# A decoder layer's expert stage: row numbers and gates on GpSimd, the gate as the scale of each dot product

## What is computed

```python
q = (x @ Wq.T).reshape(b, n, 2, HEADS, DIM_KEY).transpose(2, 0, 1, 3, 4)   # HEADS = 8
sim = jnp.einsum('pbnhd,hkpd->pbnhk', q, keys)                              # 128 keys
...                                          # best of the pairs: scores, indices (TOPK = 1)
A_in, B_in = in_a[indices], in_b[indices]
A_out, B_out = out_a[indices], out_b[indices]
gate = jax.nn.relu(scores)
hidden = x @ W_in.T
lin = jnp.einsum('bnd,bnhkd->bnhk', x, A_in) * gate
hidden = hidden + jnp.einsum('bnhk,bnhkd->bnd', lin, B_in)
hidden = jax.nn.gelu(hidden, approximate=False)
out = hidden @ W_out.T
lout = jnp.einsum('bnd,bnhkd->bnhk', hidden, A_out) * gate
out = out + jnp.einsum('bnhk,bnhkd->bnd', lout, B_out)
```

## Time and profile before

| | us |
|---|---|
| median of 3 runs | 2556.84 |
| lowest and highest | 2553.26, 2561.50 |
| span of the profiled execution | 2553.4 |
| VectorE busy in the span | 2042.5 (80%) |
| TensorE busy in the span | 2402.2 (94%) |
| GpSimd busy in the span | 1079.4 (42%) |

### The profile page before, as it was taken

One profiled execution on the slowest core, in us unless ns is written; L12 is line 12 of the kernel. 1 busy time (PEld: TensorE's weight loads), 2 busy tenths in 40 slices (PEclk: granted clock), 3 DMA queues, 4 the chain that ended last, 5 costly groups with the idle time before them and its releaser, 6 DMA issues. The chain is left out here.

```text
span 2553.4 us, 40781 instructions
## 1 busy us (share of the span) xinstructions
PE 2402.2 (94%) x12856; PEld 1333.3 (52%) x12856; DVE 2042.5 (80%) x5966; ACT 1121.9 (44%) x2612; POOL 1079.4 (42%) x1564
## 2 busy tenths in 40 slices
PE   7889999999999999999989899999999999999985
PEld 5456666656666566666555344444444444444432
DVE  1467776677767776677665699999999999999997
ACT  2257666667666666667666122222122222212221
POOL 1133333333333333334233445555555555555552
PEclk9999999999999999999999999999999999999998
DMA  3035554455545545455458789999999999999996
GB/s 112 15 108 139 163 151 141 134 148 149 155 125 144 162 143 155 114 145 172 135 148 258 272 337 390 392 382 384 382 382 383 385 389 391 383 383 382 385 371 261
DMA packets 292741, 622.47 MB, mean 244 GB/s; under 512 B 162352, under 2 KB 163376, under 8 KB 292528
## 3 DMA queue, kind: packets, MB, share of 16 engines
q0 software_dynamic: 83968, 438.34, 45.2%
q1 hardware_dynamic: 174768, 80.85, 11.9%
q10 hardware_dynamic: 33792, 100.67, 11.7%
HBM read 577.80 MB, written 142.61 MB: 282 GB/s over the span
## 5 line engine op out<-in xcount | busy, mean ns | idle before, releaser
L1544 POOL DMA_INDIRECT out_rows<-rows_out,rows_now x256 | 272.0, 1063 | 373.1 <-PE out_ps L1611 292.5
L1054 ACT ACTIVATE in_rows<-scores,nmx 128x512 f32<-128x512 f32 x512 | 373.2, 729 | 113.8 <-DVE nmx L1243 111.1
L1565 PE MATMUL l_bank<-fold,xn_tf 128*128 128x512 f32 x960 | 421.6, 592 | 0.0
L1060 ACT COPY in_rows<-t_bank 128x512 f32<-128x512 f32 x512 | 298.7, 584 | 214.7 <-PE t_bank L715 213.7
L1535 POOL DMA_INDIRECT in_rows<-rows_in,rows_now x248 | 303.2, 1223 | 128.9 <-DVE hid L1799 63.8
L622 POOL TENSOR_TENSOR added<-mask_add,band 128x136 f32<-128x136 f32 (+1 forms) x512 | 246.7, 483 | 256.4 <-DVE nmx L1243 255.0
L715 PE MATMUL t_bank<-ident,in_rows 128*128 128x128 f32 x2048 | 319.6, 281 | 10.1 <-ACT in_rows L1027 5.1
L715 PEld LDWEIGHTS t_bank<-ident,in_rows 128*128 128x128 f32 x2048 | 237.4, 143 | 171.6 <-issue 100.8
L683 PE MATMUL a_bank<-fold 128*128 128x256 f32 (+1 forms) x1024 | 303.9, 441 | 15.4 <-ACT fold L975 6.9
L1807 DVE CUSTOM_DVE_ANT_0 out_rows<-out_rows,hid 128x1024 f32<-128x1024 f32 x256 | 307.1, 1221 | 3.5 <-ACT hid L1668 3.5
L1655 ACT COPY sims<-l_bank 128x512 f32<-128x512 f32 x120 | 70.2, 585 | 537.2 <-PE l_bank L1565 516.9
(11 more groups left out here) (210 smaller groups left out, 3829.9 us busy)
## 6 DMA issues: line engine op xcount, KB each, us to landing
rows_in<-in_in_b_dram ACTq DMA_DIRECT2D x16, 2048.0 KB, 8.5
rows_out<-in_out_a_dram ACTq DMA_DIRECT2D x16, 2048.0 KB, 9.0
rows_in<-in_in_a_dram ACTq DMA_DIRECT2D x16, 1024.0 KB, 8.3
rows_out<-in_out_b_dram ACTq DMA_DIRECT2D x16, 1024.0 KB, 5.8
rel_scratch<-rel_pad SPq DMA_DIRECT2D x16, 640.0 KB, 3.2
band<-rel_scratch SPq DMA_DIRECT2D x512, 20.0 KB, 2.5
prob_scratch<-in_rows SPq DMA_DIRECT2D x512, 20.0 KB, 2.3
near<-prob_scratch SPq DMA_DIRECT2D x64, 156.1 KB, 3.1
```

The source lines that it names most:

```text
L1054: nc.scalar.activation(prob_tile(s % PSLOTS), scores[:, s % 2, :], ACT.Exp, bias=nmx[:, s:s + 1], scale=-1.0, accum_out=lsum[:, s:s + 1]). ...
L1060: nc.scalar.copy(prob_t[:, n // HPT % 2, n % HPT, :, :].rearrange("p k q -> p (k q)"), bank[:]).then_inc(t_emptied, 1)
L1544: nc.gpsimd.indirect_dma_start(out_rows[:, h, :], None, rows_out, bass.IndirectOffsetOnAxis(rows_now[:, odd, h:h + 1], 0)).then_inc(out_lo ...
L1565: ins = nc.tensor.matmul(l_bank[c % 2][:], xn_t[:, k, :], fold[:, k, c * BANK:(c + 1) * BANK], start=(k == 0), stop=(k == KD - 1))
```

## The change

Row numbers, score sums and gates are no longer made on VectorE. GpSimd makes them in a new `pick`, in six instructions on 128x8 (the multiply-and-add of the row number is now a multiply, a conversion and an addition), with waits on a counter `row_step` of its own. It stands between the input gathers of a round and its output gathers, and serves the next round. `gates` and `rows_now` now have four places, as many as the ring of tokens, and the copy of `rows` is gone.

The five multiplies by the gate are gone too. Each of the 16 products takes `gates[:, slot, h:h + 1]`, one value per partition, as its scale, where it had the constant 1.0. ScalarE's diagonals and VectorE's sums wait on the counters of the products themselves. ScalarE's first diagonal needs two products where it needed three and a multiply. The row numbers of the very first round are written by VectorE straight into `rows_now`.

```diff
--- before.py
+++ after.py
@@ -81,11 +81,12 @@
+        self.row_x = sb("row_x", [P, HEADS])
+        self.row_y = sb("row_y", [P, HEADS])
...
-        self.rows = sb("rows", [P, HEADS], U32)
...
-        self.gates = sb("gates", [P, 2, HEADS])
-        self.rows_now = sb("rows_now", [P, 2, HEADS], U32)
+        self.gates = sb("gates", [P, self.RING, HEADS])
+        self.rows_now = sb("rows_now", [P, self.RING, HEADS], U32)
@@ -1330,7 +1328,7 @@
-                nc.vector.tensor_scalar(early.rows[:], early.row_f[:], float(E - 1), None,
+                nc.vector.tensor_scalar(early.rows_now[:, 0, :], early.row_f[:], float(E - 1), None,
@@ -1520,13 +1511,26 @@
         def _(pool):
+            def pick(r):
+
+                pool.wait_ge(searched, r + 1)
+                nc.gpsimd.tensor_scalar(row_x[:], place[:, 0:HEADS, 0], float(KEYS), None,
+                                        ALU.mult).then_inc(row_step, 1)
+                nc.gpsimd.tensor_copy(row_y[:], place[:, HEADS:PH, 0]).then_inc(row_step, 1)
+                nc.gpsimd.tensor_tensor(score[:], top[:, 0:HEADS], top[:, HEADS:PH], ALU.add).then_inc(row_step, 1)
+                pool.wait_ge(row_step, 5 * (r - 1) + 2)
+                nc.gpsimd.tensor_tensor(row_f[:], row_x[:], row_y[:], ALU.add).then_inc(row_step, 1)
+                pool.wait_ge(row_step, 5 * (r - 1) + 3)
+                wait(pool, out_a_used, (r - RING + 1) * HEADS)
+                nc.gpsimd.tensor_scalar(gates[:, r % RING, :], score[:], 0.0, None, ALU.max).then_inc(row_step, 1)
+                pool.wait_ge(row_step, 5 * r)
+                nc.gpsimd.tensor_scalar(rows_now[:, r % RING, :], row_f[:], float(E - 1), None,
+                                        ALU.min).then_inc(picked, 1)
+
...
                     pool.wait_ge(picked, r + 1)
-                    nc.gpsimd.tensor_copy(rows_now[:, odd, :], rows[:]).then_inc(rows_taken, 1)
-                    pool.wait_ge(rows_taken, r + 1)
                 for n, h in enumerate([*PE_HEADS, *VE_HEADS] if r > 0 else []):
@@ -1534,8 +1538,10 @@
-                        bass.IndirectOffsetOnAxis(rows_now[:, odd, h:h + 1], 0)).then_inc(
+                        bass.IndirectOffsetOnAxis(rows_now[:, r % RING, h:h + 1], 0)).then_inc(
...
+                if r > 0 and not nothing_after(r, 1):
+                    pick(r + 1)
@@ -1657,7 +1665,7 @@
-                act.wait_ge(lin_ready, r + 1)
+                act.wait_ge(in_a_used, r * HEADS + len(PE_HEADS))
@@ -1679,7 +1687,7 @@
-                act.wait_ge(lout_first, r + 1)
+                act.wait_ge(out_a_used, r * HEADS + len(PE_OUT))
@@ -1735,19 +1743,6 @@
-            def score_rows(r):
-                dve.wait_ge(searched, r + 1)
-                nc.vector.scalar_tensor_tensor(out=row_f[:], in0=place[:, 0:HEADS, 0], scalar=float(KEYS),
-                                               in1=place[:, HEADS:PH, 0], op0=ALU.mult, op1=ALU.add)
-                nc.vector.tensor_tensor(score[:], top[:, 0:HEADS], top[:, HEADS:PH], ALU.add).then_inc(scored, 1)
...
-            def pick(r, slot):
-                dve.wait_ge(scored, r + 1)
-                nc.vector.tensor_scalar(gates[:, slot % 2, :], score[:], 0.0, None, ALU.max)
...
-                wait(dve, rows_taken, r)
-                nc.vector.tensor_scalar(rows[:], row_f[:], float(E - 1), None, ALU.min).then_inc(picked, 1)
@@ -1759,40 +1754,26 @@
 
-            def gated(lines, r, slot, some, last):
-
-                what, used = (in_a_used, lin) if lines == "in" else (out_a_used, lout)
-                dve.wait_ge(what, r * HEADS + last)
-                return nc.vector.tensor_tensor(used[:, some], used[:, some], gates[:, slot % 2, some], ALU.mult)
-
...
                 nc.vector.tensor_tensor_reduce(out=in_a[:, at, :], in0=in_a[:, at, :], in1=xn[:, slot, :],
-                                               scale=1.0, scalar=0.0, op0=ALU.mult, op1=ALU.add,
+                                               scale=gates[:, slot, h:h + 1], scalar=0.0, op0=ALU.mult, op1=ALU.add,
                                                accum_out=lin[:, h:h + 1]).then_inc(in_a_used, 1)
...
                 dve.wait_ge(xn_loaded[slot], 16 * filled(r, slot))
-                for h in PE_HEADS:
-                    product_in(r, slot, h)
-                product_in(r, slot, VE_HEADS[0])
-                gated("in", r, slot, slice(PE_HEADS[0], HEADS), len(PE_HEADS)).then_inc(lin_ready, 1)
-                for h in VE_HEADS[1:]:
+                dve.wait_ge(picked, r + 1)
+                for h in (*PE_HEADS, *VE_HEADS):
                     product_in(r, slot, h)
...
                         search_bank(nc, dve, early, 1, c, h_bank[c - 2])
-                    score_rows(1)
-                    pick(1, 1)
-
-            def gate_rest(r, slot):
-                gated("in", r, slot, slice(0, len(VE_HEADS)), HEADS).then_inc(lin_gated, 1)
 
...
                 if h == VE_HEADS[0]:
-                    dve.wait_ge(lin_gated, r + 1)
+                    dve.wait_ge(in_a_used, (r + 1) * HEADS)
                     dve.wait_ge(hid_filled, r + 1)
@@ -1800,25 +1781,25 @@
-            def product_out(r, h):
+            def product_out(r, slot, h):
...
-                                               scale=1.0, scalar=0.0, op0=ALU.mult, op1=ALU.add,
+                                               scale=gates[:, slot, h:h + 1], scalar=0.0, op0=ALU.mult, op1=ALU.add,
...
-                    dve.wait_ge(lout_gated, 2 * r + 1)
+                    dve.wait_ge(out_a_used, r * HEADS + len(PE_OUT) + FREE_OUT)
...
-                    dve.wait_ge(lout_gated, 2 * r + 2)
+                    dve.wait_ge(out_a_used, (r + 1) * HEADS)
@@ -1836,15 +1817,15 @@
-                    gate_rest(r, slot)
...
+                        dve.wait_ge(picked, 2)
...
+                    dve.wait_ge(picked, r + 2)
...
-                    gate_rest(r, slot)
@@ -1863,23 +1844,12 @@
                     search(r + 2, range(3, CHUNKS))
-                for h in PE_OUT:
-                    product_out(r, h)
-                if not nothing_after(r, 2):
-                    score_rows(r + 2)
-                product_out(r, 0)
-                gated("out", r, slot, slice(PE_OUT[0], HEADS), len(PE_OUT)).then_inc(lout_first, 1)
-                for h in range(1, FREE_OUT + 1):
-                    product_out(r, h)
-                gated("out", r, slot, slice(0, FREE_OUT), len(PE_OUT) + FREE_OUT).then_inc(lout_gated, 1)
+                for h in (*PE_OUT, *VE_OUT[:FREE_OUT + 1]):
+                    product_out(r, slot, h)
                 for h in VE_OUT[FREE_OUT + 1:]:
-                    product_out(r, h)
+                    product_out(r, slot, h)
                     if h <= 2 * FREE_OUT:
                         sum_out(r, h - FREE_OUT - 1)
-                gated("out", r, slot, slice(FREE_OUT, len(VE_OUT)), HEADS).then_inc(lout_gated, 1)
-                if not nothing_after(r, 2):
-                    dve.wait_ge(lout_gated, 2 * r + 2)
-                    pick(r + 2, slot)
                 for h in VE_OUT[FREE_OUT:]:
```

More of the change, by code:

```diff
@@ L100, in __init__ @@
         self.next_filled = sem("next_filled")
-        self.rows_taken = sem("rows_taken")
         self.in_loaded = [sem(f"in_loaded{i}") for i in range(HEADS + len(self.PE_HEADS))]
@@ L628, in early_gather @@
                 pool.wait_ge(early.picked, 1)
-                nc.gpsimd.tensor_copy(early.rows_now[:, 0, :], early.rows[:]).then_inc(early.rows_taken, 1)
-                pool.wait_ge(early.rows_taken, 1)
                 pool.wait_ge(rows_laid, 4 * 16 * B)
@@ L1417, in expert_pass @@
         xn, xn_t, xn_kept = early.xn, early.xn_t, early.xn_kept
-        top, place, row_f, rows, score, gates = (early.top, early.place, early.row_f, early.rows, early.score,
-                                                 early.gates)
-        rows_now, in_rows, rows_taken, in_loaded = early.rows_now, early.in_rows, early.rows_taken, early.in_loaded
+        top, place, row_x, row_y, row_f, score, gates = (early.top, early.place, early.row_x, early.row_y,
+                                                         early.row_f, early.score, early.gates)
+        rows_now, in_rows, in_loaded = early.rows_now, early.in_rows, early.in_loaded
         xn_loaded, w_in_loaded = early.xn_loaded, early.w_in_loaded
-        topped, searched, scored, picked = early.topped, early.searched, early.scored, early.picked
+        topped, searched, picked = early.topped, early.searched, early.picked
         w_out = sb("w_out", [P, KF, D])
@@ L1453, in expert_pass @@
         out_b_used = sem("out_b_used")
-        lin_ready = sem("lin_ready")
-        lin_gated = sem("lin_gated")
-        lout_gated = sem("lout_gated")
-        lout_first = sem("lout_first")
+        row_step = sem("row_step")
         diag_out_ready = sem("diag_out_ready")
@@ L1469, in nothing_after @@
         def nothing_after(r, ahead):
-            return isinstance(r, int) and r + ahead >= ROUNDS
```

(7 more changed lines are left out.)

## The result

| | before | after |
|---|---|---|
| median of 20 runs each | 2553.00 us | 2558.53 us |
| lowest and highest | 2550.15, 2561.50 | 2553.42, 2562.23 |
| span of the profiled execution | 2553.4 us | 2557.2 us |

The ratio is 1.0019, with a 95% interval of 1.0012 to 1.0026. The changed kernel is slower, by 4.9 us of 2553 (3.1 to 6.6 by the interval; the two medians lie 5.5 apart), about half of the forecast 9.5. The time lies inside the range, the sign is right, and the size is not: it took 20 runs each to tell 0.19% from nothing.

A forecast was written before the change was run, and what follows sets the result against it. VectorE was taken as the bound: +1.07 - 0.72 = +0.35 us over 30 rounds, +10.5, and -1 for the last two rounds, made +9.5 us and, with 3.4 carried over the span, 2566 us; range 2549 to 2579.

The forecast's parts named there:

- What bounds the kernel: Expert stage: a round of 34.10 us is the sum of what VectorE issues, until another engine takes over.
- What leaves VectorE, 0.72 us: Nine small instructions a round leave VectorE, valued by distances between starts: 0.08 + 0.14 + 0.14 + 0.36 us.
- rival 3: VectorE's nine small instructions are worth their listed time, 1.46 us: 0.39 us a round gained, 2545 us; chance 0.02.
- What comes, 1.07 us: All 16 products a round on VectorE read their scale from memory, at 0.067 us each.
- net 0.35: A full round on VectorE grows by 1.07 - 0.72 = +0.35 us, +10.5 us over 30 rounds.
- The assumption that width and place do not matter: VectorE's 1024-wide products, and the scale's place, cost the same 0.067 us as the initial value in the `bqk` row.
- GpSimd: Six 128x8 instructions a round fit before the first output gather in 7.3 us, costing VectorE nothing.
- rival 4: GpSimd's six small instructions hold VectorE: +9 us more (2575) at 0.05 us each, 2602 at 0.2; chance 0.10.
- rival 5: Gates or rows arrive late and VectorE waits for `picked`: 2570 to 2600 us; chance 0.02.
- The first two rounds, +0.7: Rounds 0 and 1 of the expert stage: forecast to be 0.7 us longer.
- The last two rounds, -1: Last two rounds: ScalarE's diagonal comes about 0.5 us earlier, output products cost some 0.2 more; about -1 us for both.
- The starting value: Median of the runs before, 2556.84 us, 3.4 us above the profiled span of 2553.4 and carried over.

The follow-up runs named there:

- kernel with other operand kinds: Kernel before, with input products' initial value and output products' initial value and scale read from memory instead of constants: 2595.02 us against 2552.36 before.
- wide pair: Changed kernel plus two spare GpSimd instructions a round, each adding two 128x128 tiles: 2569.94 us against 2556.94 for the kernel before.
- kernel with two more: Changed kernel plus two spare 128x8 GpSimd instructions a round ahead of its six: 2559.39 us against 2552.36 for the kernel before.

## Where the prediction was right, and the step that failed

- **What bounds the kernel.** Right. VectorE without idle time sets the round; every kernel above whose round moved did so by VectorE's sum, down to TensorE's cap.
- **What leaves VectorE, 0.72 us.** Right. The round grew by 0.235 us with 0.97 us added, so 0.735 left. The multiply behind the first maximum was worth nothing, as told: the 0.72 us there are unchanged. Small instructions were not worth their listed 1.46 us (rival 3), which the rule of the Trainium skill in "VectorE: DVE Perf Modes", section "The DRAIN you can't avoid", would have given; the runs are against it here, and go with what the same section adds, that an instruction which is not held starts earlier.
- **What comes, 1.07 us: this is the step that failed.** The price per operand, 0.067, was taken over from the `bqk` instructions of the first stage, by a single pair that starts 0.68 us apart. Between 224 pairs of the changed kernel's input products the distances read 0.67 (170 times), 0.68 (49) and 0.66 (5), 0.672 on average. The operand costs 0.672 - 0.611 = 0.061 us, on the wide products 1.206 - 1.145 = 0.061. Sixteen are 0.97, not 1.07. The 0.10 us a round are only a tenth of that term, but nearly a third of the net 0.35, and over 28 rounds they make 2.8 of the 4.65 us by which the forecast was too large. The single pair is a third of this error at most. The read-out of a product starts when the next product can, so each of the 32 `bqk` instructions gives a distance in the trace before; 23 read 0.68, as this one does, and 9 read 0.67:

```profile
90.86 0.75 DVE L1156 CUSTOM_DVE_ANT_0 w_in<-fold,u_row,bqk 128x512 f32<-128x512 f32 x1
91.54 0.08 DVE L1156 DVE_READ_ACCUMULATOR2_ANT row_bias<- 128x1 f32 x1
```

  Their mean is 0.677, which gives 0.065 to 0.066 an operand and 1.04 to 1.05 us a round. The rest is that the row itself is dearer: 0.677 against the 0.672 of the products that the forecast was about, in the trace before and in that after alike, and 752 ns against 748. Why an instruction of the same kind and width takes 0.005 us more there stays open.
- **The assumption that width and place do not matter.** Right, shown by the kernel with other operand kinds.
- **GpSimd.** Right: six instructions in 7.2 us (7.3 forecast), the wait for TensorE down to 1.11, no hold on VectorE (rival 4), nothing late (rival 5). The reason for "nothing" was the width, which the wide pair confirms at 0.14 us, against the 0.2 of the earlier trace rows. At those 0.2 us, the price that the prediction set beside the rule in "GPSIMD Engine Reference" of the Trainium skill, section "Specifications", this term would have been 30 us. The contention that the rule tells of is there on both sides, but VectorE pays for wide instructions and not for narrow ones. That the six would end with hardly a microsecond to spare was the wrong reading of that wait: twelve more fit.
- **The first two rounds, +0.7.** Measured +0.15; the sum of a full round was used for rounds that also wait for other engines. Round 0 is 0.68 us longer and round 1 is 0.53 shorter: there VectorE is idle ahead of its first sum, 3.31 us before and 2.54 after, and that wait takes up most of what was added. Mis-sized by 0.55 us.
- **The last two rounds, -1.** Measured -1.9. The matmuls that need the diagonal start 2.88 and 2.87 us behind the last addition of the round ahead of them, where it was 3.46 and 3.44: 0.6 us each, for the 0.5 that was forecast, and the wait for the diagonal fell from 9.79 to 9.04 us and from 7.89 to 7.45. The rest is the clock: these matmuls follow a long wait, and how long they take differs from profile to profile. Before, after, and the kernel with two more (start:end, length, busy of TensorE, its weight loads, VectorE, ScalarE, GpSimd, granted clock, DMA):

```profile
2487.41:2494.02 6.61, 6.61 (x8) 2.53 (x8) 2.38 (x9) 0.66 (x1) 3.50 (x4) 0.55 1.00 407
2520.86:2526.11 5.25, 5.25 (x8) 2.08 (x8) 2.38 (x9) 0.65 (x1) 2.44 (x3) 0.70 1.00 405
```

```profile
2492.43:2498.37 5.94, 5.93 (x8) 2.28 (x8) 3.20 (x10) 0.65 (x1) 4.06 (x4) 0.62 1.01 400
2524.76:2529.89 5.13, 5.13 (x8) 2.04 (x8) 3.20 (x10) 0.65 (x1) 3.12 (x3) 0.71 1.01 385
```

```profile
2491.19:2496.61 5.42, 5.42 (x8) 2.08 (x8) 3.19 (x10) 0.65 (x1) 4.05 (x4) 0.68 1.02 412
2523.00:2529.57 6.57, 6.57 (x8) 2.52 (x8) 3.20 (x10) 0.66 (x1) 3.13 (x3) 0.56 1.01 393
```

The same eight matmuls take 3.60 us at a granted clock of 1.00 and 5.1 to 6.6 at 0.55 to 0.71, that is, for part of the stretch at the lower of the clock's two levels (1.2 and 2.4 GHz). Of the 0.9 us by which the last rounds beat the forecast, 0.8 are this (6.61 to 5.94, 5.25 to 5.13). The kernel with two more has 5.42 and 6.57 in the same places, so I take it for scatter and not for an effect of the change.

- **The starting value.** The forecast of 2566 us was built on the median of three runs, 2556.84; twenty runs have 2553.00. Of the 7.5 us between 2566 and the measured 2558.53, 3.8 are this, and only the rest is the change.

So the mechanism held in each part, and the forecast was twice too large because it was the small difference of two terms near 1 us. Its excess of 4.65 us over the profiles' 4.85 is 2.8 us for the operands, 0.4 for what leaves VectorE (0.735 a round instead of 0.72), 0.55 for the first two rounds and 0.9 for the last two.

## What to carry to other kernels

A [P,1] operand from memory is not free on an engine that is the bound: here 0.06 us per instruction, whatever the width, so that folding one small multiply (0.08 us) into several products is a loss. Moving small work to a GpSimd with time to spare did pay (0.32 us a round), as long as it stayed narrow. And when a forecast is the small difference of two terms, read each from many rows and not from one pair. That alone would not have been enough here, because the rows stood for another line of the kernel and were themselves 0.005 us off. So widen the middle of the range by what the last digit of a borrowed price is worth in the final sum, here 0.005 us times 16 times 30, 2.4 us, and take the starting value from more than three runs.

## What the runs showed of the hardware that I had not expected

- A GpSimd instruction of 8 columns is bound to the kind of VectorE instruction beside it: 0.20 us beside a sum with an input in PSUM, 0.7 beside a sum of 0.75 us and 1.2 beside a product of 1.28 us with both inputs in SBUF.
- A gather that GpSimd issues 0.09 us behind the start of a sum of that last kind makes the sum 0.81 us long instead of 0.75 in 20 of 28 rounds; in the other 8 the gather takes 1.47 us instead of 0.94.
- GpSimd took eighteen small instructions a round instead of six with the round unchanged at 34.35 us, though in the changed kernel its waits for other engines came to under 4 us (0.85, 1.11 and 1.78 in one round) and the eighteen took 12.35.
- Behind a wait of 7 to 10 us TensorE's granted clock was between 0.55 and 0.71 in the same two places of three kernels, and the same eight matmuls took 5.13 to 6.61 us there, up to 1.4 us apart in one place.
